# A graph network's last pass: another row order, four chunks with split operands, splits placed 14 ticks ahead

## The reference

```python
agg = adj @ x;  x = layernorm(x + relu(agg @ kernel + bias))        # pass 0
u, v = x, v_node_feats
for _ in range(3):                                                  # passes 1 to 5 (the last u isn't needed)
    v = mlp(adj @ u, uv_W1, uv_b1, uv_W2, uv_b2, uv_W3, uv_b3)      # three layers, leaky relu after each
    u = mlp(adj @ v, vu_W1, vu_b1, vu_W2, vu_b2, vu_W3, vu_b3)
return layernorm(x + v)
```

## Time and profile before

| | us |
|---|---|
| median of 3 runs (1168.66 to 1168.98) | 1168.94 |
| the profiled execution | 1168.49 |
| its span | 1166.7 |
| PE busy | 1153.5 |
| DVE busy | 736.7 |
| ACT busy | 659.3 |

### The profile page before, as it was taken

The page is one execution under the profiler, slowest core; times in us unless marked ns, Lnnn a source line. Parts: engine busy times, 40 slices in busy tenths (PEclk is TensorE's granted clock), DMA queues, the critical chain, the costliest instruction groups (busy, mean ns, idle before and its releaser), DMA issues.

```text
span 1166.7 us, 13724 instructions
## 1 busy us (share of the span) xinstructions
PE 1153.5 (99%) x5242; PEld 954.0 (82%) x5242; DVE 736.7 (63%) x888; ACT 659.3 (57%) x811; POOL 4.9 (0%) x10
## 2 busy tenths in 40 slices
PE   7999999999999999999999999999999999999998
PEld 6888888888888888888888888888888888887876
DVE  7997676458555555555545746553566554678985
ACT  7765555346554555555444755553556544667874
POOL 0000000000000000000000000000000000000001
PEclk9999999999999999999999999999999999999999
DMA  9988786568356646555656636655575656579971
GB/s 383 405 301 322 251 270 198 200 216 288 120 205 217 210 157 213 199 195 181 205 188 220 238 124 211 205 179 198 192 242 165 212 186 230 166 292 356 312 281 36
DMA packets 72353, 261.60 MB, mean 224 GB/s; under 512 B 8032, under 2 KB 8800, under 8 KB 71264
## 3 DMA queue, kind: packets, MB, share of 16 engines
q1 hardware_dynamic: 72144, 260.61, 64.0%
q10 hardware_dynamic: 144, 0.13, 0.0%
HBM read 258.61 MB, written 2.10 MB: 223 GB/s over the span
## 4 chain that ended last, share of the span: by engine, by line
PE 94%; DMA 3%; DVE 1%; ACT 0%; SPq 0%; issue 0%; ACTq 0%
PE agg_ps L932 29%; PE agg_ps L925 28%; PE agg_ps L918 28%; PE pre_ps L829 4%; DMA adj_raw<-in_adj 3%; PE hid_ps L790 1%; PE hid_ps L792 1%; PE hid_ps L791 1%; DVE adj_lo L770 1%; PE hid_ps L851 1%; PE hid_ps L865 0%; ACT adj_hi L635 0%; DVE stats L648 0%; PE hid_ps L868 0%; SPq L496 0%
## 5 line engine op out<-in xcount | busy, mean ns | idle before, releaser
L770 DVE TENSOR_TENSOR adj_lo<-adj_raw,adj_hi 128x1024 fp32r<-128x1024 f32 x464 | 547.8, 1219 | 224.9 <-ACT adj_hi L635 219.6
L918 PE MATMUL agg_ps<-adj_hi,feat_hi 128*128 128x512 f32 x1484 | 586.4, 395 | 7.5 <-ACT adj_hi L635 7.5
L925 PE MATMUL agg_ps<-adj_hi,feat_lo 128*128 128x512 f32 x1484 | 579.3, 390 | 0.0
L635 ACT ACTIVATE adj_hi<-adj_raw 128x1024 fp32r<-128x1024 f32 x464 | 467.6, 1051 | 83.3 <-PE agg_ps L932 69.1
L932 PE MATMUL agg_ps<-adj_lo,feat_hi 128*128 128x512 f32 x1484 | 458.8, 390 | 0.2 <-DVE adj_lo L770 0.2
L918 PEld LDWEIGHTS agg_ps<-adj_hi,feat_hi 128*128 128x128 f32 x1484 | 279.6, 188 | 66.0 <-issue 9.4
L925 PEld LDWEIGHTS agg_ps<-adj_hi,feat_lo 128*128 128x128 f32 x1484 | 279.5, 188 | 59.1 <-issue 1.9
L932 PEld LDWEIGHTS agg_ps<-adj_lo,feat_hi 128*128 128x128 f32 x1484 | 278.9, 188 | 59.5 <-DVE adj_lo L770 1.1
L528 ACT ACTIVATE hid<-hid_ps,params 128x512 f32<-128x512 f32 (+2 forms) x82 | 55.1, 672 | 59.6 <-PE hid_ps L792 50.7
L600 ACT ACTIVATE in_hi<-part 128x512 fp32r<-128x512 f32 x24 | 15.2, 634 | 110.3 <-DVE part L759 110.3
L528 ACT ACTIVATE post<-pre 128x512 f32<-128x512 f32 x39 | 24.7, 632 | 88.0 <-DVE pre L737 88.0
(11 more groups left out here) (80 smaller groups left out, 389.8 us busy)
## 6 DMA issues: line engine op xcount, KB each, us to landing
adj_raw<-in_adj SPq DMA_DIRECT2D x472, 512.0 KB, 5.6
adj_raw<-in_adj SPq DMA_DIRECT2D x8, 1024.0 KB, 8.1
resid<-in_x SPq DMA_DIRECT2D x8, 256.0 KB, 8.1
out<-resid SPq DMA_DIRECT2D x7, 256.0 KB, 5.3
params<-in_weights SPq DMA_DIRECT2D x1, 386.0 KB, 5.1
b_row<-in_bias_rows SPq DMA_DIRECT2D x1, 128.0 KB, 5.7
out<-resid SPq DMA_DIRECT2D x2, 64.0 KB, 1.8
out<-resid ACTq DMA_DIRECT2D x1, 128.0 KB, 1.9
```

The costliest lines, as they stand in the source:

```text
L635: act.activation(split_hi(b)[:, i * CHUNK:(i + pieces) * CHUNK], adj_raw[:, h % RAW, 0:pieces * CHUNK], ACT.Copy).then_inc(adj_hi_ready, 1)
L770: dve.tensor_tensor(split_lo(b)[:, slot], adj_raw[:, h % RAW, 0:pieces * CHUNK], split_hi(b)[:, slot].bitcast(F32), ALU.subtract).then_inc ...
L918: pe.matmul(group_bank(g), feat_hi[feats][:, tile(src, i)], split_hi(b)[:, piece(i)], start=start, stop=False)
L925: pe.matmul(group_bank(g), feat_lo[feats][:, tile(src, i)], split_hi(b)[:, piece(i)], start=False, stop=False)
```

## The change

Four things change together:

1. `LAST_ROWS` is (6, 1, 5, 4, 3, 2) and was (6, 5, 4, 3, 1, 2): the row of two blocks comes second and not second to last.
2. The first four chunks of the last pass, (5, 0), (5, 7), (5, 6) and (5, 1), are a new kind LAST_PARTS and computed in parts, with longer distances between the steps. LATE3 goes, and LATE2 and LATE get other distances.
3. `LAST_LEAD` is 14 and was 20.
4. Row 7 of pass 4 is worked off as in the passes before it: (7,0) to (7,3) with both products, FINISH of (7,4) to (7,7), then BEGIN of (7,4) to (7,6), whose blocks stay in the ring for it. It was FINISH of (7,7), then (7,0) to (7,6) with both products each.

```diff
-LEAD, FIRST_LEAD, LAST_LEAD, FIRST_ROWS = 12, 4, 20, 3
+LEAD, FIRST_LEAD, LAST_LEAD, FIRST_ROWS = 12, 4, 14, 3
...
+    LAST_PARTS: dict(dve_sum=0, act_in=3, dve_in=4, pe_hid1=10, act_hid1=11, dve_hid=13, pe_hid2=20, act_hid2=21,
+                     pe_out=25, dve_pre=25, act_post=28, dve_stats=29, act_std=32, dve_shift=33, act_norm=36),
     LAST: dict(dve_sum=0, act_in=0, pe_hid1=6, act_hid1=7, pe_hid2=10, act_hid2=11, pe_out=14, dve_pre=14,
                act_post=16, dve_stats=16, act_std=20, dve_shift=20, act_norm=24),
-    LATE3: dict(dve_sum=0, act_in=0, pe_hid1=6, act_hid1=7, pe_hid2=10, act_hid2=11, pe_out=14, dve_pre=14,
-                act_post=16, dve_stats=17, act_std=20, dve_shift=20, act_norm=24),
-    LATE2: dict(dve_sum=0, act_in=1, pe_hid1=4, act_hid1=5, pe_hid2=7, act_hid2=8, pe_out=9, dve_pre=10,
-                act_post=10, dve_stats=12, act_std=14, dve_shift=15, act_norm=16),
-    LATE: dict(dve_sum=0, act_in=1, pe_hid1=1, act_hid1=2, pe_hid2=3, act_hid2=5, pe_out=5, dve_pre=7, act_post=7,
-               dve_front=8, dve_total=8, dve_stats=9, act_std=12, dve_root=13, pool_norm=13),
+    LATE2: dict(dve_sum=0, act_in=0, pe_hid1=5, act_hid1=6, pe_hid2=9, act_hid2=10, pe_out=13, dve_pre=13,
+                act_post=14, dve_stats=15, act_std=18, dve_shift=18, act_norm=22),
+    LATE: dict(dve_sum=0, act_in=1, pe_hid1=3, act_hid1=4, pe_hid2=5, act_hid2=7, pe_out=7, dve_pre=9, act_post=9,
+               dve_front=10, dve_total=10, dve_stats=11, act_std=14, dve_root=15, pool_norm=15),
...
-LAST_ROWS = (6, 5, 4, 3, 1, 2)
+LAST_IN_PARTS = 4
+LAST_ROWS = (6, 1, 5, 4, 3, 2)
...
+        yield from both(s, top, range(top - 3))
+        yield from finish(s, top, range(top - 3, rows))
+        yield from begin(s, top, range(top - 3, top))
         if s < PASSES - 2:
-            yield from both(s, top, range(top - 3))
-            yield from finish(s, top, range(top - 3, rows))
-            yield from begin(s, top, range(top - 3, top))
             for r in EARLY:
                 yield from finish(s + 1, r, (r,))
             yield from finish(s + 1, 0, (0,))
-        else:
-            yield from finish(s, top, (top,))
-            yield from both(s, top, range(top))
...
-                else LATE3 if after == 3 else LAST
+                else LAST_PARTS if u < self.rows * (PASSES - 1) + LAST_IN_PARTS else LAST
...
-        return self.steps_of(u) in (IN_PARTS, TURN)
+        return self.steps_of(u) in (IN_PARTS, TURN, LAST_PARTS)
...
-                u = at(t, "dve_hid", HIDDEN)
+                u = at(t, "dve_hid", DEEP)
...
-                u = at(t, "dve_in", HIDDEN)
+                u = at(t, "dve_in", DEEP)
```

More of the change, by code:

```diff
@@ L40 @@
 HOLD = 3
-LEAD, FIRST_LEAD, LAST_LEAD, FIRST_ROWS = 12, 4, 20, 3
+LEAD, FIRST_LEAD, LAST_LEAD, FIRST_ROWS = 12, 4, 14, 3
 LOAD_GCN, LOAD_PARAMS = 24, 90
 W_SPLIT = 320
-IN_PARTS, TURN, LATE3, LATE2, LATE, END, END2 = "in_parts", "turn", "late3", "late2", "late", "end", "end2"
+IN_PARTS, TURN, LAST_PARTS, LATE2, LATE, END, END2 = "in_parts", "turn", "last_parts", "late2", "late", "end", "end2"
 STEPS = {
```

## The result

The changed kernel takes **1174.72 us** (median, 1174.41 to 1175.0) beside 1168.78 us (1168.54 to 1168.98) of the kernel before on the same chip: a ratio of 1.0051, 95% interval 1.0038 to 1.0065, or 5.9 us more. The profiled execution took 1174.54 us with a span of 1172.7. In the kernel after, everything from L65 on stands two lines higher: L918 is now L916, L790 to L792 are L788 to L790, L770 is L768.

A forecast was written before the change was run, and what follows sets the result against it. DVE's list was to replace PE as bound from 1061.5 us: 81.0 us work, 11.0 handover gaps, 1.0 crossings, 93.0 against 86.4, so 6.6 more. Profiled 1168.49 + 6.6 = 1175.1, plus 0.45 for the median: 1175.5 us, range 1168.5 to 1181.

The forecast's parts named there:

- PE's side: From 1061.5 us to the LATE hidden layer, PE alone would need 84.5 us instead of 86.4, a gain of 1.9.
- PE stays the only bound: Rival, chance 0.08: DVE's handovers fall below 3.5 us, all removed PE work shows, 1.9 us faster, 1167.0 us.
- work and idle time of DVE: From 1061.5 us to the LATE sum: 81.0 us of work plus 12.0 of gaps, 93.0 in all.
- I take them to remain: In the last pass, DVE's 11.0 us of handover gaps, waiting for ACT or PE, were to stay.
- the rival of absorbed handovers: Rival, chance 0.12: a late DVE waits less, 3 to 6 of 11 us of gaps stay, 1167.0 to 1171.2 us.
- The eight new crossings: Added DVE waits for ACT from the chunks in parts, put at 1.0 us for all eight, ends 0 and 8.
- the three splits and the lead: Lead 14 puts three more splits, 3.4 us, after 1061.5 us and gives away 4.1 us of stock, causing the wait.
- the turn at nothing: New order of row 7 in pass 4 costs 0, bounds 0 and 2.2 us, as it is free in passes 1 to 3.
- DVE's list as the bound: From 1061.5 us DVE's list sets the end, 6.6 us later; this case, +2.3 to +12 us, had chance 0.70.

The follow-up runs named there:

- the run with light DVE work: Changed kernel, but VectorE subtracts only the first 512 of 1024 columns of each last-pass split: 1167.05 us.
- the GpSimd run: Changed kernel with six of the eight added subtractions moved from VectorE to GpSimd: 1175.27 us.
- the narrow subtractions: Changed kernel, but each of the eight added VectorE subtractions works on 64 of 512 columns: 1173.61 us.
- the narrow copies: Changed kernel, but ScalarE writes only 64 of 512 columns of `in_hi` and `hid_hi` for the four chunks: 1173.22 us.

## Why the prediction was right, and where it wasn't

Forecast were 1175.5 us, range 1168.5 to 1181, and 6.6 us more than before; measured are 1174.72 and 5.9 more.

**Right: PE's side.** 84.5 us for PE alone, 1.9 us on offer; the run with light DVE work shows 1.7. Had DVE and ACT kept up, this would have been the result. In the kernel as it is the rival "PE stays the only bound" is refuted: with PE busiest of all and its work cut, the time went up by 5.9 us.

**Right in its sums: work and idle time of DVE.** Forecast 81.0 us of work and 12.0 of gaps, 93.0 in all; measured 79.8 and 12.6, 92.4. The tail is unchanged, its DVE work 2.0 us less, as the moved statistics of LATE2 ask. PE's waits are 7.7 us in all between (5, 6) and (5, 3), forecast some 8, on the hidden copies and `part` sums named, with `hid_lo` as one I hadn't named and none for `pre`, which I had. `act_hid1` of (5, 5) queued behind `act_post` of (5, 1) is the longest. ScalarE in order of time, after:

```profile
1121.99 1.65 ACT L547 ACTIVATE resid<-post,shift,rstd 128x128 f32<-128x128 f32 x4 [0.93 <-DVE shift L693]
...
1124.49 0.61 ACT L526 ACTIVATE post<-pre 128x512 f32<-128x512 f32 x1
...
1125.96 0.67 ACT L526 ACTIVATE hid<-hid_ps,params 128x512 f32<-128x512 f32 x1
```

That last activation ends at 1126.6, and PE starts at 1126.68 after 2.17 us. DVE between 1075 and 1145 us is busy 89% and not over 90%.

**Wrong: "I take them to remain".** The sum of the gaps held, not their make-up. Of the 11.0 us before, 2.7 were waits for PE (7.6 less the 4.9 at the end); they vanished, just as the rival of absorbed handovers says. The 8.0 us of waits for ACT grew to 12.0. The eight new crossings, costed at 1.0 in DVE's gaps, show 0.0 at their own place; the growth stands before splits. Two errors of 3 and 3 us (gaps that go; waits for ACT that grow by 4.0 and not by 1.0) cancel, and that they do is luck: the forecast of 1175.5 came within 0.8 us by it. The constant is none: the change made DVE's waits for ACT half as long again, and a later `act_std` nearly doubled them once more, to 22.0 us, with the same instructions.

**Wrong: the three splits and the lead.** "With 14, the engines stop at a step with 6 ticks less done in advance" is refuted: undoing it costs 0.9 us more. The splits done ahead of 1061.5 are 440 or 441 with either lead, so the 3.4 us charged to the lead are not its doing. The term is about as large as it was put, again by luck: 48 half-blocks were split in the stretch and not 46, 57.8 us of recorded rows beside 54.3. DVE's load before 1061.5 was to fall by them; it rose from 25.88 to 30.43 us, mostly through the turn (29.31 with the turn alone). The stretch did begin two half-blocks poorer than before (440 against 442), through the turn as well (440 with it alone, 441 with the chunks in parts alone). Nor did a short stock matter by itself: no split of the kernel after was ready less than 6.5 us before its use (12.4 before). What the lag delays is the chunk steps that stand between the splits.

**Wrong by its condition: the turn at nothing.** It is nearly free with a lead of 14 (0.1 us) and costs 1.3 to 1.4 with 20, inside the bounds of 0 and 2.2. The cover I named, the same turn in earlier passes with a lead of 12, was the right row; I didn't see that the lead was a condition of it.

**Wrong: DVE's list as the bound.** The prediction charges the added crossings and then treats DVE as a single list of 93 us. 3.6 us off it bring 1.1; 6.2 us off ACT, which the prediction puts at "less than DVE", bring 3.7. What binds is the chain that both form.

**Open:** the share of the row order. Without chunks in parts it costs nothing that shows; with them it and the lead account for some 1.7 us that the runs don't divide. Whether the third and fourth chunk cost so much for their number or for their place is open too. A version of the change that keeps all the work and beats the kernel before wasn't found: with none, two or four chunks in parts the times are 1168.95, 1169.49 and 1174.72.

## What to carry to other kernels

When two helper engines run fixed lists and wait for each other several times for every item, look at their mutual waits, both directions summed, and not at their busy shares. With no chunk in parts DVE and ACT were busy for 87% and 80% of a stretch in which PE didn't wait until its last 0.3 us; with four they were busy for 86% and 76%, and PE lost 7.7 us. The mutual waits were 22.6 us before, 19.8 with no chunk in parts, 22.1 with two and 29.4 with four. The sum is a sign and no price: with 3.6 us less work on DVE it is 29.5, and the kernel 1.1 us faster. Before you take 0.2 us from the main engine by giving the helpers two more crossings, ask how much room the chain of both has, and expect a price that isn't even (0.5 us for the first two chunks, 5.2 for the next two). Moving a step to relieve one crossing tightens the neighbours, so check who stands behind whom on both lists first.

## What the hardware showed that I had not expected

**The clock after a wait.** After 2.17 us in which PE waited for `act_hid1` of (5, 5), the granted clock stayed at 1.00 in the kernel after; after 2.14 us at the same place with a lead of 20 it fell. The stretches around that wait, first after, then lead 20:

```profile
1124.00:1130.00 6.00, 3.83 (x16) 2.48 (x15) 5.07 (x12) 4.30 (x7) 0.00 (x0) 1.00 0.89 289
```

```profile
1125.00:1130.00 5.00, 2.86 (x7) 1.36 (x6) 3.80 (x7) 3.88 (x5) 0.00 (x0) 0.81 0.78 275
```

TensorE in order of time with a lead of 20: the two instructions of the hidden layer take 1.95 us and not the 1.12 of the kernel after, and matmuls follow 0.43 us apart (1130.16 to 1130.59) and not 0.23, about the lower of the two levels of 1.2 and 2.4 GHz, for a few microseconds:

```profile
1127.98 1.95 PE L849 MATMUL hid_ps<-hid,params 128*128 128x512 f32 x2 [2.14 <-ACT hid L526]
1128.95 1.42 PE L916 MATMUL agg_ps<-feat_hi 128*128 128x512 f32 x1
1130.16 0.63 PE L923 MATMUL agg_ps<-feat_hi,feat_lo 128*128 128x512 f32 x1
1130.59 0.63 PE L916 MATMUL agg_ps<-feat_hi 128*128 128x512 f32 x1
```

Which of the two happens the recorded waits don't tell. The clock fell too after 2.13 us (the GpSimd run, 0.58 over 1128 to 1131 us), 2.14 (the narrow subtractions, 0.60 over the same) and 2.28 (the kernel before with chunks in parts, 0.59 over 1125 to 1128), and after 4.2 with the later `act_std` (0.88 over 1126 to 1140); it stayed after 2.08 with the narrow copies. Its cost differs. In the kernel before with chunks in parts PE didn't wait again up to the LATE sum, and the time was lost. With a lead of 20 it cost nothing in the end. PE is 1.30 us behind the kernel after at this hidden layer (1127.98 and 1126.68) and still 1.30 at the first one of (5, 4) (1142.46 and 1141.16), because PE's wait there is 0.8 us shorter.

**GpSimd beside VectorE.** A subtraction of 128x512 took 1.29 to 1.40 us on GpSimd in five of six cases and 2.29 in one; on VectorE it takes 0.69. In this run the two overlap each time, and the longer times are those of instructions that began second. GpSimd's of 2.29 us began 0.05 us after a split subtraction of VectorE. Three split subtractions of VectorE that began beside one of GpSimd took 1.53 to 1.55 us and not 1.22. Two VectorE instructions on 4 columns took 1.18 and 1.04 us where they take 0.16 elsewhere, and ended within 0.03 us of GpSimd's. Not every one is held up: VectorE's reciprocal at 1102.19 kept its 0.17. The experiment with GpSimd, VectorE first, then GpSimd:

```profile
1090.97 1.18 DVE L693 SCALAR_TENSOR_TENSOR shift<-mean_var,rstd 128x4 f32<-128x4 f32 x1
...
1102.40 1.04 DVE L693 SCALAR_TENSOR_TENSOR shift<-mean_var,rstd 128x4 f32<-128x4 f32 x1
```

```profile
1090.84 1.29 POOL L778 TENSOR_TENSOR in_lo<-part,in_hi 128x512 fp32r<-128x512 f32 x1 [10.45 <-ACT in_hi L598]
...
1102.01 1.40 POOL L782 TENSOR_TENSOR hid_lo<-hid,hid_hi 128x512 fp32r<-128x512 f32 x1 [9.88 <-ACT hid L526]
1103.41 2.29 POOL L778 TENSOR_TENSOR in_lo<-part,in_hi 128x512 fp32r<-128x512 f32 x1
```
